# Two running sums in DRAM in place of three, for the routed rows of a mixture-of-experts layer

## The chip, the cores and the metric

The kernel runs on one core of one Trainium2 chip. The metric is device time in microseconds (us), the median of several executions. A core has five engines that run their own instruction streams and meet only at semaphores: TensorE (PE, with its weight loads as PEld), VectorE (DVE), ScalarE (ACT), GpSimd (POOL) and SyncE (SP), and 16 DMA engines that they all share.

## The reference

`x` has 32 batches of 100 rows of 256 numbers, 3200 tokens in all, float32. First a cross attention over a context of 361 rows of 192 is added to it. Then comes the part that matters here, a feed-forward layer with a router:

```
h = layernorm(x)
aff = softmax(h @ Wr + br)                  # 31 experts
vals, idx = top_k(aff, 3)
gates[token, expert] = vals where chosen, else 0
shared = gelu(h @ ws1 + bs1) @ ws2 + bs2
routed = sum over experts e of gates[:, e] * (gelu(h @ We1[e] + Be1[e]) @ We2[e] + Be2[e])
out = x + shared + routed + h
```

Each token has three experts. So 9600 rows have to be gathered by expert, multiplied, and added back to their tokens.

## The kernel before

**Attention stage.** Steps `i` from -2 to 36 run a pipeline over the 32 batches. For each finished tile of 128 tokens (25 tiles) it writes two rows per token into DRAM arrays of 3328 rows (3200 tokens and 128 rows for padding) of 256 floats: the residual into `sums[0]` (L370) and the normed row `h` into `sums[1]` (L371), both on SyncE's queue. GpSimd scatters `h` three times (L530) into `xs`, a DRAM array ordered by expert. At step 24 SyncE writes zeros from `pad_rows` into the whole of a third array, `sums[2]` (L349, one DMA of 3328 KB), and into the padding rows of the other two (L352, two DMAs of 128 KB). `spare_ready` counts these three.

**Routed stage.** 105 tiles of 128 rows, each of one expert, partly or wholly padding towards the end of the list. For each tile `t`:

- SyncE loads 128 rows with what belongs to them from `xs` into one of `XS = 6` buffers `xt` (L430), when `y_sb` of tile t-6 has been made.
- TensorE transposes them (L1176), forms the up product (L1187) and the down product (L1198), in the order transposes of t+2, up of t+1, down of t. ScalarE copies the transposed rows (L677) and applies gelu (L651).
- VectorE copies the token numbers of the rows to `token` (L934), fetches the weights of tile t+2 (L917), and evacuates the down product, scaled by the gate, to one of 6 `y_sb` buffers (L925). Before L934 it waits until the add of tile t-6 has landed (L933).
- GpSimd adds the 128 rows of `y_sb` to a sum in DRAM at the rows named in `token` (L552, an indirect DMA with `compute_op=ADD`). Sums are taken in turn. Two tiles of different experts can hold the same token, so the kernel never has two adds to one sum in flight: an add waits until the last add to the same sum has landed:

```python
s, sx = t.slot(3), t.slot(XS)
pool.wait_ge(token_ready, t.count(1))
pool.wait_ge(y_made, t.count(S_E + 1))
if t.has(3):
    pool.wait_ge(added[s], adds(t, 3))
alone(pool)
```

`alone` (L84) is a no-op that keeps these waits apart from the DMA instruction. After adds t = 1, 4, 7, ... up to 31, GpSimd also issues a plain DMA that pads the list of an expert (L559). SyncE issues 20 such pads (L416) between its loads.

**Tail.** When all adds have landed (L442), SyncE loads the sums in 11 groups of tiles (L448 to L450, one DMA of each sum for each group, into `part0`, `part1`, `part2`, which lie over the spent weights). VectorE adds the second and the third to the first (L959, L962). To tiles 0 to 7 it adds the shared expert's result, made early and kept in `tok` (L966). For the 17 others (`late_tiles`) TensorE forms the shared product after the routed tiles (L1106, L1115, L1116) into six PSUM banks, and VectorE adds it from there (L972). The product of late tile k from k = 6 on waits for the final sum of late tile k-6, whose bank it takes (L1223). After all loads are issued, SyncE writes the groups out (L453) as they are final.

Of the kernel before, what the change touches and what calls it, by code (L numbers as in the profile page):

```python
# [13 lines left out]
F32 = mybir.dt.float32  # L14
# [3 lines left out]
ALU = mybir.AluOpType  # L18
# [3 lines left out]
P = 128  # L22
B, LQ, LK = 32, 100, 361
D1, D2, E = 256, 192, 256
# [8 lines left out]
TOKENS = B * LQ  # L33
TILES = TOKENS // P
# [46 lines left out]
def alone(eng):  # L81


    eng.nop(nofuse=True)  # L84
# [18 lines left out]
GROUPS = [(8, 11), (0, 1), (11, 14), (1, 3), (14, 17), (3, 5), (17, 20), (5, 7), (20, 23), (7, 8), (23, 25)]  # L103


def starts(i):
    return FIRST.index(i) if i in FIRST else None


def ends(i):  # L110
    return LAST.index(i) if i in LAST else None


def batch(i):
    return i if 0 <= i < B else None
# [7 lines left out]
def program(nc, x, ctx_t, cols, rows, wqt, wkt, wvt, wo, bo, w1, be1, w2, b2, wr, br, out):  # L123
    xs = nc.dram_tensor("expert_rows_in", [LIST_END + P, ROW], F32, kind="Internal").ap()


    sums = [nc.dram_tensor(f"sum{k}", [TOKENS + P, D1], F32, kind="Internal").ap() for k in range(3)]
    flat_x = x.rearrange("b t d -> (b t) d")
    flat_out = out.rearrange("b t d -> (b t) d")

# [1 line left out]
    with stack:  # L132
        def sb(name, shape, dt=F32):
            return stack.enter_context(nc.sbuf_tensor(name, shape, dt))
# [7 lines left out]
        def sems(*names):  # L142
            return [stack.enter_context(nc.semaphore(n)) for n in names]

        XS = 6
        NT = ROUTED_TILES
        W = XS
        w1_all = sb("w1_all", [P, NE + 1, 2 * INTER])
        w2_all = sb("w2_all", [P, NE + 1, 2 * D1])
# [11 lines left out]
        pad_rows = sb("pad_rows", [P, ROW])  # L161
# [57 lines left out]
        token = ring(XS, "token", [P, 1], I32)  # L219
        own_exp, gate, inverse = two("own_exp", [P, TOP]), two("gate", [P, 1]), two("inverse", [P, 1])  # L220
        part0, part1 = w1_all[:, 0:TILES, 0:D1], w1_all[:, 0:TILES, D1:2 * D1]
        part2 = w2_all[:, 0:TILES, 0:D1]


        zt_ps0, zt_ps1 = bank[2], bank[3]
# [35 lines left out]
            "counts_made", "late_steps", "pads_ready", "pads_out", "pool_pads_out", "diag_made", "table_spread", "table_made",  # L261
            "gates_transposed", "gates_t_copied", "spare_ready")
        tile_in = sems(*[f"tile_in{s}" for s in range(XS)])
        added = sems("added0", "added1", "added2")
        (tile_transposed, tile_t_copied, w1_ready, up_made, act_made, down_made, y_made, token_ready, picked,
         inverse_made, gate_made) = sems(
            "tile_transposed", "tile_t_copied", "w1_ready", "up_made", "act_made", "down_made", "y_made", "token_ready",
            "picked", "inverse_made", "gate_made")
        rows_in = sems(*[f"rows_in{g}" for g in range(len(GROUPS))])
        third_in = sems(*[f"third_in{g}" for g in range(len(GROUPS))])  # L270
        sum_made, final_made, final_out = sems("sum_made", "final_made", "final_out")

        MADE = 23
# [21 lines left out]
        def cut(t):  # L295
            return slice(t * P, t * P + P)
# [12 lines left out]

        def adds(t, back=0):  # L310

            return t.turn(3, 1 - back // 3) * 16

        block = stack.enter_context(nc.Block())

# [1 line left out]
        def _(sp):  # L317
# [23 lines left out]
            def step(i):  # L341
                if batch(i + 4) is not None:
                    load_ctx(i + 4)
                if starts(i + 4) is not None:
                    load_x(starts(i + 4))
                if i == FILL_STEP:
                    sp.wait_ge(made, MADE)
                    alone(sp)
                    sp.dma_start(sums[2].rearrange("(k p) n -> p k n", p=P),  # L349
                                 pad_rows[:, 0:D1].unsqueeze(1).to_broadcast([P, TILES + 1, D1])).then_inc(spare_ready, 16)  # L350
                    for k in range(2):
                        sp.dma_start(sums[k][TOKENS:TOKENS + P, :], pad_rows[:, 0:D1]).then_inc(spare_ready, 16)  # L352
                    sp.dma_start(xs[LIST_END:LIST_END + P, :], pad_rows[:, :]).then_inc(pads_out, 16)
                if i == FILL_STEP + 2:
                    sp.dma_start(w1_all[:, NE, :], w1[NE]).then_inc(shared_in, 16)
                    sp.dma_start(w2_all[:, NE, :], w2[NE]).then_inc(shared_in, 16)
                if 1 <= i <= len(w1_order):
                    e = w1_order[i - 1]
                    sp.dma_start(w1_all[:, e, :], w1[e]).then_inc(expert_in, 16)
                if 1 <= i <= len(w2_order):  # L360
                    e = w2_order[i - 1]
                    if i == 1:
                        sp.wait_ge(folds_ready, 1)
                        alone(sp)
                    sp.dma_start(w2_all[:, e, :], w2[e]).then_inc(expert_in, 16)
                t = ends(i - 4)
                if t is not None:
                    sp.wait_ge(h_made, t + 1)
                    alone(sp)
                    sp.dma_start(sums[0][cut(t), :], resid[t % SLOTS][:, :]).then_inc(base_out[t % SLOTS], 16)  # L370
                    sp.dma_start(sums[1][cut(t), :], h_sb[t % SLOTS][:, 0:D1]).then_inc(h_out[t % SLOTS], 16)  # L371
# [66 lines left out]
            for t in range(FULL_FIRST, NT):  # L438
                load(At(0, t, W))

            for s in range(3):
                sp.wait_ge(added[s], len(range(s, NT, 3)) * 16)  # L442

            def rows_of(dram, lo, hi):
                return dram[lo * P:hi * P, :].rearrange("(k p) n -> p k n", p=P)

            for g, (lo, hi) in enumerate(GROUPS):
                sp.dma_start(part0[:, lo:hi, :], rows_of(sums[0], lo, hi)).then_inc(rows_in[g], 16)  # L448
                sp.dma_start(part1[:, lo:hi, :], rows_of(sums[1], lo, hi)).then_inc(rows_in[g], 16)
                sp.dma_start(part2[:, lo:hi, :], rows_of(sums[2], lo, hi)).then_inc(third_in[g], 16)  # L450
            for g, (lo, hi) in enumerate(GROUPS):
                sp.wait_ge(final_made, final_at[hi - 1])
                sp.dma_start(rows_of(flat_out, lo, hi), part0[:, lo:hi, :]).then_inc(final_out, 16)  # L453
# [3 lines left out]
        def _(pool):  # L457
            n = [0]

            def const(ins):  # L460
# [6 lines left out]
            k = const(pool.memset(tri[:, :], 1.0))  # L467
            pool.wait_ge(made, k)
            k = const(pool.affine_select(out=ident[:, :], in_=ident[:, :], compare_op=ALU.not_equal, fill=1.0,
                                         base=0, pattern=[[-1, P]], channel_multiplier=1))  # L470
# [24 lines left out]
            k = const(pool.memset(gates_all[:, TILES:28, :], 0.0))  # L495
# [42 lines left out]
            for s in range(SLOTS):  # L538
                pool.wait_ge(base_out[s], len(range(s, TILES, SLOTS)) * 16)
                pool.wait_ge(h_out[s], len(range(s, TILES, SLOTS)) * 16)  # L540
            pool.wait_ge(spare_ready, 48)

            def add(t):


                s, sx = t.slot(3), t.slot(XS)
                pool.wait_ge(token_ready, t.count(1))
                pool.wait_ge(y_made, t.count(S_E + 1))
                if t.has(3):
                    pool.wait_ge(added[s], adds(t, 3))  # L550
                alone(pool)
                pool.indirect_dma_start(sums[s], bass.IndirectOffsetOnAxis(ap=token[sx][:, 0:1], axis=0),  # L552
                                        y_sb[sx][:, :], None, compute_op=ALU.add).then_inc(added[s], 16)
# [140 lines left out]
        def _(dve):  # L694
# [233 lines left out]
            def tile(t, more=True):  # L928

                s, sx = t.slot(2), t.slot(XS)  # L930
                dve.wait_ge(tile_in[sx], t.turn(XS, 1) * 16)
                if t.has(XS):
                    dve.wait_ge(added[t.slot(3)], adds(t, XS))  # L933
                dve.tensor_copy(token[sx][:, :], xt[sx][:, TOKEN:TOKEN + 1]).then_inc(token_ready, 1)  # L934
                dve.scalar_tensor_tensor(own_exp[s][:, :], xt[sx][:, WHO:WHO + TOP], tile_e[:, t.r:t.r + 1],
                                         xt[sx][:, EXPS:EXPS + TOP], ALU.is_equal, ALU.mult).then_inc(picked, 1)
                dve.reciprocal(inverse[s][:, :], xt[sx][:, SUM:SUM + 1]).then_inc(inverse_made, 1)
                if more:
                    fetch_w1(t.back(-2))
                dve.wait_ge(picked, t.count(1))  # L940
                dve.tensor_reduce(gate[s][:, :], own_exp[s][:, :], AX.X, ALU.add).then_inc(gate_made, 1)
                evac(t)
# [14 lines left out]
            for g, (lo, hi) in enumerate(GROUPS):  # L957
                dve.wait_ge(rows_in[g], 32)
                dve.tensor_tensor(part0[:, lo:hi, :], part0[:, lo:hi, :], part1[:, lo:hi, :], ALU.add).then_inc(sum_made, 1)  # L959
                dve.wait_ge(sum_made, 2 * g + 1)  # L960
                dve.wait_ge(third_in[g], 16)
                dve.tensor_tensor(part0[:, lo:hi, :], part0[:, lo:hi, :], part2[:, lo:hi, :], ALU.add).then_inc(sum_made, 1)  # L962
                dve.wait_ge(sum_made, 2 * g + 2)
                if lo < S_E:
                    rows = part0[:, lo:hi, :].rearrange("p k (c q) -> p k c q", c=2)
                    dve.tensor_tensor(rows, rows, tok[:, :, lo * P:hi * P].rearrange("p c (k q) -> p k c q", q=P),  # L966
                                      ALU.add).then_inc(final_made, 1)
                else:
                    for t in range(lo, hi):
                        k = late_tiles.index(t)  # L970
                        dve.wait_ge(down_made, S_E + NT + k + 1)
                        dve.tensor_tensor(part0[:, t, :], part0[:, t, :], last_ps[k % 6], ALU.add).then_inc(final_made, 1)  # L972
# [299 lines left out]
```

## Time and profile before

| what | value |
|---|---|
| device time, median of 3 runs | 512.31 us (511.34 to 512.83) |
| span of the profiled execution | 515.6 us |
| PE busy | 473.5 us, 92% |
| POOL busy | 321.6 us, 62% |
| DVE busy | 349.8 us, 68% |
| adds L552 | 105, first at 262.3, last at 471.4 us |
| SyncE's wait at L442 for the last adds | 16.5 us |

The profiled execution is one execution, 3.3 us longer than the median of the unprofiled runs. Times in the views are counted from its first instruction. A share of busy time says little by itself: the three stages (attention up to some 242 us, routed tiles to 475 us, tail to 515.6 us) have different limits, and each is to be read for itself.

### The profile page before, as it was taken

What the parts mean: (1) busy time and instruction counts of PE and PEld (TensorE: products, weight loads), DVE (VectorE), ACT (ScalarE), POOL (GpSimd) and SP (SyncE); (2) the same over time, 40 slices, a digit from 0 to 9 for tenths busy, and PEclk for the clock granted to TensorE, in tenths of its full rate; (3) what the DMA queues carried; (4) which work ended last, traced back from release to release, by engine and by line L of the source; (5) the groups of instructions that cost most, each with busy time, mean ns of one, the idle gap of its engine ahead of it and who ended that gap; (6) DMA issues with size and microseconds to landing.
All of it is one profiled execution on the core that took longest, in us unless ns stands there. A gap on an engine that the chain in (4) does not pass through costs nothing.

```text
span 515.6 us, 13640 instructions
## 1 busy us (share of the span) xinstructions
PE 473.5 (92%) x3248; PEld 414.0 (80%) x3248; DVE 349.8 (68%) x1555; ACT 247.2 (48%) x823; POOL 321.6 (62%) x356
## 2 busy tenths in 40 slices
PE   8699888889888998888899999999999999999991
PEld 7577767778677787777799899989999999999891
DVE  4858787785878858657557666666666666661784
ACT  1455646465455555546255454454555555553220
POOL 3224856757565755657158888878888888885000
PEclk9899989999899889999999999999999999999996
DMA  7645767675555972569359999998998888875999
GB/s 238 178 145 180 244 211 231 219 231 181 190 181 166 348 246 93 165 203 329 90 121 186 190 183 179 191 151 135 138 137 143 138 135 137 137 117 65 350 350 316
DMA packets 81150, 97.53 MB, mean 189 GB/s; under 512 B 9201, under 2 KB 65906, under 8 KB 81074
## 3 DMA queue, kind: packets, MB, share of 16 engines
q1 hardware_dynamic: 60786, 70.79, 46.0%
q0 software_dynamic: 19248, 25.40, 29.6%
q10 hardware_dynamic: 1040, 0.48, 0.5%
q8 instruction: 29, 0.48, 0.4%
q14 instruction: 47, 0.39, 0.3%
HBM read 54.91 MB, written 41.73 MB: 187 GB/s over the span
## 4 chain that ended last, share of the span: by engine, by line
PE 49%; issue 15%; DVE 10%; DMA 8%; SPq 4%; POOL 3%; ACT 1%; POOLq 0%; DVEq 0%; another core or an unknown queue 0%
PE bank L1187 9%; PE bank L1198 9%; DMA sum<-y_sb,token 5%; POOL sum L552 3%; PE bank L1056 3%; PE bank L1045 3%; PE bank L1044 3%; PE bank L1176 2%; PE bank L1059 2%; PE bank L1083 2%; PE bank L1082 2%; DMA w_all<-sum 2%; DVE w_all L740 2%; PE bank L1031 2%; PE bank L1074 1%
## 5 line engine op out<-in xcount | busy, mean ns | idle before, releaser
L552 POOL DMA_INDIRECT sum<-y_sb,token x105 | 170.3, 1622 | 48.5 <-issue 26.7
L651 ACT ACTIVATE up<-bank,b_all 128x128 f32<-128x128 f32 x260 | 81.2, 363 | 103.0 <-PE bank L1187 44.8
L1187 PE MATMUL bank<-xtt,w1b 128*128 128x128 f32 x840 | 111.1, 275 | 0.3 <-ACT xtt L677 0.3
L1198 PE MATMUL bank<-w_all,up 128*128 x420 | 108.6, 381 | 0.0
L1187 PEld LDWEIGHTS bank<-xtt,w1b 128*128 128x128 f32 x840 | 102.1, 192 | 0.8 <-ACT xtt L677 0.5
L925 DVE TENSOR_SCALAR y_sb<-bank,gate,inverse 128x256 f32<-128x256 f32 x105 | 57.1, 544 | 53.5 <-PE bank L1198 27.5
L530 POOL DMA_INDIRECT expert_rows_in<-xt,slot x75 | 77.0, 1027 | 26.1 <-issue 20.7
L1198 PEld LDWEIGHTS bank<-w_all,up 128*128 128x128 f32 x420 | 71.7, 191 | 5.7
L917 DVE COPY w1b<-w_all 128x512 f32 x105 | 47.5, 452 | 19.1 <-issue 9.2
L677 ACT ACTIVATE xtt<-bank 128x256 f32<-128x256 f32 x105 | 40.1, 383 | 38.5 <-issue 21.4
L1176 PE MATMUL bank<-ident,xt 128*128 128x128 f32 x210 | 40.1, 274 | 0.4 <-DMA xt<-expert_rows_in 0.3
L1176 PEld LDWEIGHTS bank<-ident,xt 128*128 128x128 f32 x210 | 29.2, 141 | 12.0 <-DMA xt<-expert_rows_in 1.4
L608 ACT ACTIVATE tok<-bank 128x100 f32<-128x100 f32 x32 | 8.1, 253 | 58.2 <-PE bank L1059 52.1
L1056 PEld LDWEIGHTS bank<-w_all 128*128 128x128 f32 (+1 forms) x192 | 27.9, 200 | 10.1 <-issue 2.3
L505 POOL TENSOR_TENSOR rs<-mv,eps_cols 128x4 f32<-128x4 f32 x32 | 6.6, 207 | 45.1 <-DVE mv L777 44.7
L507 POOL TENSOR_TENSOR rs<-rs,mhalf 128x4 f32<-128x4 f32 x32 | 33.0, 1032 | 2.5
L740 DVE TENSOR_SCALAR w_all<-w_all,mv,rs 128x192 f32<-128x192 f32 x96 | 31.4, 384 | 1.6 <-POOL rs L507 1.3
L1044 PE MATMUL bank<-w_all,tok 128*100 128x361 f32 x64 | 27.7, 517 | 0.4 <-issue 0.4
L1056 PE MATMUL bank<-w_all 128*128 128x100 f32 (+1 forms) x192 | 27.0, 278 | 0.8 <-ACT w_all L589 0.8
L703 DVE BATCH_NORM_STATS2 c<-w_all 128x6 f32<-128x192 f32 x96 | 27.3, 341 | 0.0
L790 DVE RECIPROCAL rinv<-bank 128x1 f32<-128x1 f32 x25 | 4.2, 167 | 34.2 <-PE bank L1083 30.5
L1045 PE MATMUL bank<-w_all,tok 65*100 65x361 f32 x64 | 27.3, 510 | 0.0
(179 smaller groups left out, 939.1 us busy)
## 6 DMA issues: line engine op xcount, KB each, us to landing
xt<-expert_rows_in SPq DMA_DIRECT2D x105, 132.0 KB
w_all<-in_w SPq DMA_DIRECT2D x47, 256.0 KB
w_all<-in_ctx SPq DMA_DIRECT2D x32, 288.0 KB
w_all<-sum SPq DMA_DIRECT2D x15, 384.0 KB, 7.6
sum<-pad_rows SPq DMA_DIRECT2D x1, 3328.0 KB
w_all<-in_x SPq DMA_DIRECT2D x25, 128.0 KB, 2.9
sum<-y_sb SPq DMA_DIRECT2D x25, 128.0 KB
sum<-xt SPq DMA_DIRECT2D x25, 128.0 KB
```

Source lines behind the costliest of these rows:

```text
L530: pool.indirect_dma_start(xs, bass.IndirectOffsetOnAxis(ap=slot[s4][:, k:k + 1], axis=0), h_sb[s4][:, :], None).then_inc(scattered[s4], 16)
L552: pool.indirect_dma_start(sums[s], bass.IndirectOffsetOnAxis(ap=token[sx][:, 0:1], axis=0), y_sb[sx][:, :], None, compute_op=ALU.add).then ...
L651: ins = act.activation(up[s][:, m * P:m * P + P], up_ps[s][:, m * P:m * P + P], ACT.Gelu, bias=b1_all[:, e, m:m + 1].rearrange("p o n -> p ...
L740: ins = dve.tensor_scalar(z[s4][:, k, 0:D2], c_sb[s4][:, k, :], mv[s][:, k, 0:1], rs[s][:, 1, k:k + 1], ALU.subtract, ALU.mult)
L917: dve.tensor_copy(w1b[n.slot(2)][:, :], w1_all[:, bass.ds(e, 1), :].rearrange("p o n -> p (o n)"))\
L925: dve.tensor_scalar(y_sb[sx][:, :], down_ps[s], gate[s][:, 0:1], inverse[s][:, 0:1], ALU.mult, ALU.mult).then_inc(y_made, 1)
L1044: pe.matmul(bank[s][0:LQ, 0:LK], tok[:, 0, of_batch(b)], zt0[s], start=True, stop=False)
L1045: pe.matmul(bank[s][0:LQ, 0:LK], tok[0:D2C, 1, of_batch(b)], zt1[s], start=False, stop=True)\
L1056: pe.matmul(mix_ps[:, 0:LQ], z[s4][0:KT[k], k, 0:P], probs_t[s][0:KT[k], k, :], start=(k == 0), stop=(k == 2))
L1176: mm = pe.transpose(tile_ps[s][:, c * P:c * P + P], xt[sx][:, c * P:c * P + P], ident[:, :])
L1187: mm = pe.matmul(up_ps[s][:, m * P:m * P + P], w[:, c * INTER + m * P:c * INTER + m * P + P], xtt[s][:, c * P:c * P + P], start=(c == 0), ...
L1198: mm = pe.matmul(down_ps[s], up[s][:, m * P:m * P + P], w, start=(m == 0), stop=(m == 1))
```

## The change

The routed rows are added in turn to two sums, the one that begins as the residual and the one that begins as `h`. The third sum is neither allocated, filled with zeros, loaded nor added. The wait ahead of an add is now for the add two tiles back in place of three.

```diff
-    sums = [nc.dram_tensor(f"sum{k}", [TOKENS + P, D1], F32, kind="Internal").ap() for k in range(3)]
+    sums = [nc.dram_tensor(f"sum{k}", [TOKENS + P, D1], F32, kind="Internal").ap() for k in range(2)]
...
         def adds(t, back=0):
 
-            return t.turn(3, 1 - back // 3) * 16
+            return t.turn(2, 1 - back // 2) * 16
...
-                    sp.dma_start(sums[2].rearrange("(k p) n -> p k n", p=P),
-                                 pad_rows[:, 0:D1].unsqueeze(1).to_broadcast([P, TILES + 1, D1])).then_inc(spare_ready, 16)
                     for k in range(2):
                         sp.dma_start(sums[k][TOKENS:TOKENS + P, :], pad_rows[:, 0:D1]).then_inc(spare_ready, 16)
...
-            for s in range(3):
-                sp.wait_ge(added[s], len(range(s, NT, 3)) * 16)
+            for s in range(2):
+                sp.wait_ge(added[s], len(range(s, NT, 2)) * 16)
...
                 sp.dma_start(part1[:, lo:hi, :], rows_of(sums[1], lo, hi)).then_inc(rows_in[g], 16)
-                sp.dma_start(part2[:, lo:hi, :], rows_of(sums[2], lo, hi)).then_inc(third_in[g], 16)
...
-                s, sx = t.slot(3), t.slot(XS)
+                s, sx = t.slot(2), t.slot(XS)
                 pool.wait_ge(token_ready, t.count(1))
                 pool.wait_ge(y_made, t.count(S_E + 1))
-                if t.has(3):
-                    pool.wait_ge(added[s], adds(t, 3))
+                if t.has(2):
+                    pool.wait_ge(added[s], adds(t, 2))
...
                 if t.has(XS):
-                    dve.wait_ge(added[t.slot(3)], adds(t, XS))
+                    dve.wait_ge(added[t.slot(2)], adds(t, XS))
...
                 dve.tensor_tensor(part0[:, lo:hi, :], part0[:, lo:hi, :], part1[:, lo:hi, :], ALU.add).then_inc(sum_made, 1)
-                dve.wait_ge(sum_made, 2 * g + 1)
-                dve.wait_ge(third_in[g], 16)
-                dve.tensor_tensor(part0[:, lo:hi, :], part0[:, lo:hi, :], part2[:, lo:hi, :], ALU.add).then_inc(sum_made, 1)
-                dve.wait_ge(sum_made, 2 * g + 2)
+                dve.wait_ge(sum_made, g + 1)
```

## Rows read from the trace of the kernel before

**Rows 1.** The page: span, and busy time of TensorE and the rest.

```profile
span 515.6 us, 13640 instructions
PE 473.5 (92%) x3248; PEld 414.0 (80%) x3248; DVE 349.8 (68%) x1555; ACT 247.2 (48%) x823; POOL 321.6 (62%) x356
```

**Rows 2.** Windows: length, then busy us per engine (PE first), clock, DMA share, GB/s.

```profile
262.00:332.00 70.00, 69.57 (x485) 63.06 (x484) 45.97 (x207) 34.99 (x105) 59.60 (x44) 1.00 0.93 182
332.00:384.00 52.00, 51.97 (x368) 47.68 (x368) 34.91 (x159) 26.41 (x79) 42.82 (x27) 1.00 0.92 142
384.00:475.00 91.00, 91.00 (x639) 84.07 (x639) 55.28 (x257) 44.23 (x133) 74.72 (x46) 1.00 0.82 128
475.00:515.60 40.60, 29.80 (x187) 27.09 (x185) 25.45 (x44) 8.12 (x26) 0.00 (x0) 0.90 0.99 324
```

**Rows 3.** The chain that ended last (start, us, what): up products of two routed tiles.

```profile
361.89 0.89 PE bank L1187 x8
...
363.87 0.89 PE bank L1187 x8
```

**Rows 4.** All adds of L552: ns min/median/max, first and last start.

```profile
L552 POOL DMA_INDIRECT sum<-y_sb,token x105: 1543/1606/1797, 262.3 to 471.4; - x105
```

**Rows 5.** Timeline of DVE and POOL at the second add.

```profile
262.85 0.54 DVE L925 TENSOR_SCALAR y_sb<-bank,gate,inverse 128x256 f32<-128x256 f32 x1 [0.73 <-PE bank L1198]
...
264.21 1.57 POOL L552 DMA_INDIRECT sum<-y_sb,token  x1 [0.30 <-issue]
```

**Rows 6.** Timeline of POOL: adds after a gap, adds two before, and the last two.

```profile
345.42 1.71 POOL L552 DMA_INDIRECT sum<-y_sb,token  x1 [0.30 <-issue]
348.09 1.56 POOL L552 DMA_INDIRECT sum<-y_sb,token  x1 [0.96 <-DVE y_sb L925]
...
451.86 1.68 POOL L552 DMA_INDIRECT sum<-y_sb,token  x1 [0.30 <-DMA sum<-y_sb,token]
...
458.19 1.55 POOL L552 DMA_INDIRECT sum<-y_sb,token  x1 [0.69 <-issue]
...
469.53 1.55 POOL L552 DMA_INDIRECT sum<-y_sb,token  x1 [0.30 <-issue]
471.39 1.55 POOL L552 DMA_INDIRECT sum<-y_sb,token  x1 [0.30 <-issue]
```

**Rows 7.** The chain: adds from their start to the landing.

```profile
396.49 3.94 DMA sum<-y_sb,token
...
418.25 3.79 DMA sum<-y_sb,token
...
455.82 4.18 DMA sum<-y_sb,token
...
471.39 3.81 DMA sum<-y_sb,token
```

**Rows 8.** Timeline of SyncE's queue behind the fill of the third sum.

```profile
166.69 8.30 SPq L352 DMA_DIRECT2D sum<-pad_rows  x2
```

**Rows 9.** Windows around that fill, columns as in rows 2.

```profile
170.00:175.00 5.00, 3.81 (x31) 3.10 (x29) 3.94 (x23) 2.62 (x11) 4.10 (x6) 1.00 1.06 352
175.00:180.00 5.00, 4.96 (x24) 3.85 (x25) 4.27 (x22) 1.92 (x8) 3.75 (x5) 0.64 1.03 338
```

**Rows 10.** The chain near it: the same product at either clock.

```profile
176.34 1.06 PE bank L1044 x2
...
185.55 0.61 PE bank L1044 x2
```

**Rows 11.** The tail: timeline of SyncE's queue and DVE.

```profile
475.28 0.38 SPq L448 DMA_DIRECT2D w_all<-sum  x1
...
479.86 0.96 DVE L959 TENSOR_TENSOR w_all<-w_all 128x768 f32<-128x768 f32 x1 [11.05 <-DMA w_all<-sum]
...
482.25 1.08 DVE L972 TENSOR_TENSOR w_all<-w_all,bank 128x256 f32<-128x256 f32 x3
...
508.38 0.75 DVE L972 TENSOR_TENSOR w_all<-w_all,bank 128x256 f32<-128x256 f32 x2
```

More of the change, by code:

```diff
@@ L221, in program @@
         part0, part1 = w1_all[:, 0:TILES, 0:D1], w1_all[:, 0:TILES, D1:2 * D1]
-        part2 = w2_all[:, 0:TILES, 0:D1]
         zt_ps0, zt_ps1 = bank[2], bank[3]
@@ L263, in program @@
         tile_in = sems(*[f"tile_in{s}" for s in range(XS)])
-        added = sems("added0", "added1", "added2")
+        added = sems("added0", "added1")
         (tile_transposed, tile_t_copied, w1_ready, up_made, act_made, down_made, y_made, token_ready, picked,
@@ L269, in program @@
         rows_in = sems(*[f"rows_in{g}" for g in range(len(GROUPS))])
-        third_in = sems(*[f"third_in{g}" for g in range(len(GROUPS))])
         sum_made, final_made, final_out = sems("sum_made", "final_made", "final_out")
@@ L540, in _ @@
                 pool.wait_ge(h_out[s], len(range(s, TILES, SLOTS)) * 16)
-            pool.wait_ge(spare_ready, 48)
+            pool.wait_ge(spare_ready, 32)
             def add(t):
-                s, sx = t.slot(3), t.slot(XS)
+                s, sx = t.slot(2), t.slot(XS)
                 pool.wait_ge(token_ready, t.count(1))
                 pool.wait_ge(y_made, t.count(S_E + 1))
-                if t.has(3):
-                    pool.wait_ge(added[s], adds(t, 3))
+                if t.has(2):
+                    pool.wait_ge(added[s], adds(t, 2))
                 alone(pool)
```

## The prediction

> **What bounds the kernel now.** I read the windows by stage first, since an average over three stages says nothing about one. TensorE is busy for 92% of the span [rows 1] and for all but 0.5 us of the 213 us of the routed stage, at full clock [rows 2]. The chain of waits confirms it: one routed tile is one turn of TensorE, 363.87 - 361.89 = 1.98 us [rows 3]. The adds keep the same pace: (471.39 - 262.3) / 104 = 2.01 us apart [rows 4, 6]. From 375 us on the chain runs over GpSimd instead, because the last add's landing is what the tail waits for. The tail is bound by transfers, DMA share 0.99 at 324 GB/s, with TensorE busy 29.8 of 40.6 us [rows 2].
>
> So the question is what the adds' queue can do when an add has to wait for the add two back. Two numbers decide it, the time from an add's start to its landing and the time from a release to the next start.
>
> **The loop of one sum.** Landing: the chain shows seven adds from start to landing, 3.79 to 4.18 us, mean 3.9 [rows 7]. This contains the 1.55 us that the instruction occupies GpSimd [rows 6]. Restart: the second add found GpSimd idle and waited only for `y_sb`, made at 262.85 + 0.54 = 263.39; it began at 264.21, 0.82 us later [rows 5]. A wait for a landing sits at the same place, ahead of the no-op, so I take 0.82 us for it too. Before the change this is hidden: one sum comes up every 3 x 1.98 = 5.94 us, and the loop needs 3.9 + 0.82 = 4.72. It shows only when a landing is late. The add at 458.19 comes late after even spacing, and three turns earlier the add began at 451.86 [rows 6]; if the landing released it, that landing took 458.19 - 0.82 - 451.86 = 5.51 us. The gap before 348.09 is of the same kind. Such gaps are rare, so most landings stay below 5.94 - 0.82 = 5.1 us, which is the upper bound where the chain shows none.
>
> After the change one sum comes up every 2 tiles, 3.96 us at TensorE's pace, and the loop needs 4.72. The loop becomes the bound: 4.72 / 2 = 2.36 us per tile. GpSimd's own limit, 471.39 - 469.53 = 1.86 us [rows 6], stays below, and the eleven plain pads among the early adds fit into the new idle time of about 0.5 us (partly).
>
> The seven landings lie in a window with DMA share 0.82; from 262 to 384 us it is 0.93 and 0.92 [rows 2], and no landing there is in the chain. Bounds: 3.8 us, the shortest seen, and 5.1. I take 4.2: busier engines lengthen it, yet two adds in flight in place of up to three, and a fifth fewer loads per us, shorten it. About 60 adds start there, so their pace is (4.2 + 0.82) / 2 = 2.51 us; the other 44 intervals take 2.36.
>
> Last add: 262.3 + 60 x 2.51 + 44 x 2.36 = 516.7. It lands 3.81 later [rows 7], at 520.5, against 471.39 + 3.81 = 475.2. **Routed stage: +45.3 us.**
>
> What is late next: VectorE's copy of `token` for tile t waits for the landing of add t-6, and everything behind it on that engine with it (weights of t+2, evacuation). TensorE runs out of `y_sb` buffers some six tiles in and then idles 2.4 - 1.98, about 0.5 us per tile. SyncE's load of tile t+6 waits for the same evacuation. None of these adds time: evacuation follows the landing by some 2 us, and four adds are still queued then, 4 x 2.4 us of work.
>
> At this place the Trainium skill (DMA: Bandwidth & Descriptors, section Anatomy of one DMA) gives 2.0 us plus bytes / 436 GB/s for a DMA of GpSimd, 2.3 us for these 128 KB, as an estimate. Taken as the whole loop it would hide the wait. The trace's 3.8 to 4.2 us from the start of the instruction speak against that reading: the 1.55 us on GpSimd come first.
>
> **The fill removed.** One DMA of 3328 KB disappears at 166 us, and the 8.3 us for which SyncE is held up behind it [rows 8]. I cost it at nothing. The DMA engines are full at 170 to 180 us [rows 9], but the chain there runs over TensorE and VectorE without a DMA in it. What could be gained: TensorE's clock is 0.64 on average in the window after it was busy for 3.81 of 5 us [rows 9], and the same product takes 1.06 in place of 0.61 us [rows 10]. If the fill had a part in that idling, its absence gives back up to 0.36 x 5 + 0.3 x 5, some 3 us. I keep 0 to -3, and take 0 because the chain names none of its transfers.
>
> **The tail.** 11 of 33 loads go, 3.28 of 9.83 MB. At the 350 GB/s of these transfers (352 at full share, [rows 9]) that is 9.4 us, the upper bound, as transfers fill the tail. VectorE's 11 third additions, under 1 us each (the first group's is seen between 479.86 and 482.25), go too. But then TensorE's late tiles hold the end. First loads are issued at 475.28, the first addition starts at 479.86, and the first final tile at 482.25 [rows 11], of which 0.96 + some 0.4 us belong to the third sum: after the change it comes at landing + 5.7. From there TensorE has eleven down products of 1.3 us and nine up products of 0.9 left, 22.3 us (eight matmuls of 128 columns take 0.89 us [rows 3], which is the up product; the down product with its bias has six of 256 columns, at twice the time each, 1.3). Then the last addition, about 0.8, and the last write: now 515.6 - 509.1 = 6.5 us after the last addition's end at 508.38 + 0.75 [rows 11], when the writes queue. Sum: 5.7 + 0.4 + 22.3 + 0.8 + 6.5 = 35.7 us against 515.6 - 475.2 = 40.4. With an emptier queue the last write may be 2 to 3 us shorter; but TensorE will have stood still for some 10 us before (six late tiles, 13 us, fit ahead of the landing and are done early) and may start at the low clock, costing about as much. **Tail: -5 us**, bounds -3 and -9.4.
>
> **Sum.** +45.3 - 5 + 0 = +40.3. Against its own execution: 515.6 + 40.3 = 555.9. The median of the runs is 3.3 us below the profiled execution, so 512.3 + 40.3 = 552.6 us.
>
> **The rivals.**
>
> *The clock falls in the routed stage.* TensorE will be busy for 1.98 of 2.44 us, 81%. The window with 76% ended in the low level, 1.2 GHz for part of the next stretch [rows 9]. At 1.2 GHz a tile costs 3.96 us. Short stretches of it are hidden by the four queued adds; if the mean clock came to 0.75, a tile would cost 1.98 / 0.75 = 2.64 us, and the stage 104 x (2.64 - 2.45) = 20 us more: 573 us. Against it: after the drop TensorE has no idle time, so the clock should recover. The Trainium skill (TensorE: Matmul & The Clock Gate, section The HAM clock gate) says that idleness lowers the clock and activity releases it, which could make it swing. Chance 0.10.
>
> *Landings get much shorter.* With fewer adds in flight all could land in 3.8 us or just below: 104 x 2.31 = 240.2, last add at 502.5, +31.1; with a tail of -9.4 it gives +21.7, 534 us. For it speaks that the last add, with no loads beside it, took 3.81; against it that this was no shorter than others. Chance 0.12.
>
> *Faster: the wait stays covered.* The routed stage keeps its 1.98 us, only the tail shows: 512.3 - 5 = 507 us (503 at best). This needs a loop under 3.96 us, so a landing of 3.14 after 0.82; with 5 us from the tail the balance is at 1.98 + 5/104 = 2.03 us per tile, a landing of 3.24. The shortest in the trace is 3.79 [rows 7]. Or the restart costs nothing, because the queue of GpSimd runs ahead: then (3.9 + 0) / 2 = 1.95, covered. Against this speaks the 0.82 us at 264.21 and the late add at 458.19, which fits a landing within the range only with some restart. Chance 0.04.
>
> *Landings as long as the middle of the bounds*, 4.5 early and 4.1 later: 60 x 2.66 + 44 x 2.46 = 267.8, +58.7, tail -3: 568 us. Chance 0.12.
>
> **How the numbers follow.** My forecast has 0.62, its rivals 0.10, 0.12, 0.04 and 0.12. The range takes in short and middle landings, 535 to 570 us, and leaves the clock and the covered wait outside. A measurement tells 0.3%, 1.5 us, from no change; slower by more 0.96, within 0.01, faster 0.03 (the covered wait's 0.04, in two parts).
>
> **What would show it.** The adds L552 spaced 2.3 to 2.6 us, GpSimd idle over 0.7 us before each, released by the add two back; TensorE some 80% busy from 280 us on; VectorE's L934 waiting for a landing; last add near 517 us; a tail of 34 to 37 us with TensorE in it, idle just before the landing. The prediction is wrong if adds stay 2 us apart (restart or landing hidden), if the clock column shows 0.8 or less in the routed stage, or if the stage before 250 us moves by more than 3 us.

## The result, and the profile after

The changed kernel takes 555.69 us (median of 4 runs, 553.15 to 559.36) against 511.82 us of the kernel before on the same chip: ratio 1.0823, 95% interval 1.0741 to 1.0906. It is slower by 43.9 us. The forecast was 552.6 us, 40.3 us more, with a range of 535 to 570. A second chip repeats the ratio (1.0854, 1.0785 to 1.0923), at absolute times that differ by chip.

The page of the changed kernel, beside [rows 1]. The last two lines are the head of its chain of waits, by engine and by line.

```profile
span 557.7 us, 13607 instructions
PE 492.5 (88%) x3248; PEld 421.1 (76%) x3248; DVE 346.0 (62%) x1544; ACT 248.3 (45%) x823; POOL 316.0 (57%) x356
...
PEclk9789989989899989999999999999999999999989
...
PE 34%; DMA 31%; issue 11%; DVE 10%; SPq 2%; ACT 1%; POOL 1%; DVEq 1%; POOLq 1%; another core or an unknown queue 0%
DMA sum<-y_sb,token 30%; PE bank L1036 3%; PE bank L1048 3%; PE bank L1037 3%; PE bank L1107 3%; PE bank L1051 2%; PE bank L1098 2%; PE bank L1074 2%; PE bank L1023 2%; DVE w_all L735 1%; PE bank L1088 1%; PE bank L1075 1%; PE bank L984 1%;
```

DMA transfers now hold 31% of the chain, and 30% of the span is one thing, the way of an add from its start to its landing. The windows by stage answer to [rows 2]; the columns are the same.

```profile
262.00:332.00 70.00, 64.24 (x428) 56.25 (x426) 40.50 (x180) 31.13 (x93) 46.90 (x36) 1.00 0.76 150
332.00:384.00 52.00, 45.89 (x302) 40.11 (x303) 30.06 (x129) 21.55 (x64) 35.68 (x24) 1.00 0.73 131
384.00:516.00 132.00, 116.83 (x766) 102.02 (x765) 71.66 (x316) 53.79 (x160) 84.39 (x54) 1.00 0.66 105
516.00:524.00 8.00, 8.00 (x52) 7.38 (x51) 0.00 (x0) 2.51 (x8) 4.66 (x3) 1.00 0.57 66
524.00:557.70 33.70, 25.19 (x147) 22.56 (x145) 17.34 (x33) 6.26 (x20) 0.00 (x0) 0.90 0.89 292
```

TensorE is busy for 64.24, 45.89 and 116.83 us of 70, 52 and 132, 89% in place of 100%. Its granted clock stays at 1.00 in all of the routed stage, the higher of the two levels. The DMA share fell from 0.93, 0.92 and 0.82 to 0.76, 0.73 and 0.66. So neither an engine nor the transfers are full: the stage is bound by a latency.

All adds of the changed kernel, beside [rows 4], and then its timeline of GpSimd, beside [rows 6]:

```profile
L547 POOL DMA_INDIRECT sum<-y_sb,token x105: 1544/1552/1839, 264.5 to 520.7; - x105
```

```profile
356.62 1.55 POOL L547 DMA_INDIRECT sum<-y_sb,token  x1 [0.90 <-DVE token L929]
358.83 1.55 POOL L547 DMA_INDIRECT sum<-y_sb,token  x1 [0.66 <-DVE token L929]
361.28 1.55 POOL L547 DMA_INDIRECT sum<-y_sb,token  x1 [0.90 <-DVE token L929]
363.42 1.55 POOL L547 DMA_INDIRECT sum<-y_sb,token  x1 [0.59 <-DVE token L929]
365.99 1.55 POOL L547 DMA_INDIRECT sum<-y_sb,token  x1 [1.02 <-DVE token L929]
367.97 1.55 POOL L547 DMA_INDIRECT sum<-y_sb,token  x1 [0.43 <-issue]
370.49 1.55 POOL L547 DMA_INDIRECT sum<-y_sb,token  x1 [0.97 <-DVE token L929]
```

(520.7 - 264.5) / 104 = 2.46 us from add to add, against 2.01. Every second add belongs to the same sum, 356.62, 361.28, 365.99, 370.49, so a turn takes 4.5 to 4.7 us. The view names VectorE's copy of `token` as the releaser. That is a trap: the token of tile t+4 waits for the same landing as add t, so its copy runs at the very moment at which the add is released. The add's own inputs were ready long before: by the trace's records, from the seventh add on its rows had been made over 4.1 us earlier and its own token copied over 6.0 us earlier. The chain of the changed kernel takes it apart, in order of time (start, us, what):

```profile
508.12 5.28 DMA sum<-y_sb,token
513.40 0.02 issue
513.42 0.02 POOLq L545
513.44 0.04 issue
513.48 0.04 POOLq L84
513.52 0.69 issue
514.21 3.79 DMA sum<-y_sb,token
518.00 0.02 issue
518.03 0.02 POOLq L545
518.04 0.04 issue
518.09 0.04 POOLq L84
518.13 0.69 issue
518.82 1.04 POOL sum L547
```

The landing at 513.40 lets the wait at L545 pass at once. The no-op follows, then 0.69 us until the add starts at 514.21: 0.81 us from landing to start. Then 3.79 us to the next landing, and 0.82 us again. These two terms and nothing else make up one turn.

**Where the 42.1 us of the profiled executions went** (557.7 - 515.6). The first add starts 2.2 us later (264.52 against 262.30). The 104 intervals take 256.2 in place of 209.1 us, 47.1 more. The tail, from the last landing to the end, takes 557.7 - 524.4 = 33.3 in place of 40.4 us, 7.1 less. 2.2 + 47.1 - 7.1 = 42.2.

The tail in the timeline of the changed kernel, beside [rows 11]:

```profile
524.42 0.38 SPq L444 DMA_DIRECT2D w_all<-sum  x1
...
528.98 0.96 DVE L954 TENSOR_TENSOR w_all<-w_all 128x768 f32<-128x768 f32 x1 [17.49 <-DMA w_all<-sum]
...
529.97 1.08 DVE L964 TENSOR_TENSOR w_all<-w_all,bank 128x256 f32<-128x256 f32 x3
530.45 2.07 PE L1107 MATMUL bank<-w_all,up 128*128 128x256 f32 x4 [5.52 <-DVE w_all L964]
...
534.44 1.03 PE L1107 MATMUL bank<-w_all,up 128*128 128x256 f32 x4
...
544.69 0.42 DVE L964 TENSOR_TENSOR w_all<-w_all,bank 128x256 f32<-128x256 f32 x1 [1.77 <-PE bank L1108]
...
554.74 0.42 DVE L964 TENSOR_TENSOR w_all<-w_all,bank 128x256 f32<-128x256 f32 x1 [0.80 <-PE bank L1108]
```

The first final tile begins at 529.97, 5.6 us after the landing. TensorE had run out of free banks and stood still for 5.52 us; its four matmuls at 530.45 then take 2.07 us, and 1.03 at 534.44. The windows show the clock of that stretch, and of the rest (columns as in [rows 2]):

```profile
524.93:530.45 5.52, 0.00 (x1) 0.00 (x1) 1.44 (x3) 0.63 (x2) 0.00 (x0) 0.70 0.88 292
530.45:534.00 3.55, 3.55 (x11) 3.01 (x12) 3.13 (x8) 0.00 (x0) 0.00 (x0) 0.51 1.09 353
534.00:557.70 23.70, 20.70 (x130) 18.80 (x128) 12.78 (x24) 5.64 (x18) 0.00 (x0) 1.00 0.89 295
```

The granted clock fell to the lower level, 1.2 GHz, while TensorE stood still, and was back at the higher one from 534 us on. From 544 us on VectorE waits for TensorE before its final additions, 1.77 us at 544.69, so this end of the tail is held by TensorE, no longer by transfers. The last addition ends at 555.16, and the last write is done 2.6 us later.

### The profile page after: what moved, and what is told of

The parts are those of the page before. It is cut to its first block, busy times and chain, and to the rows that moved or that the text cites. A ratio compares the mean times of both kernels' runs of the same rounds, so it can differ in the third digit from the quotient of the medians.

```text
span 557.7 us, 13607 instructions
## 1 busy us (share of the span) xinstructions
PE 492.5 (88%) x3248; PEld 421.1 (76%) x3248; DVE 346.0 (62%) x1544; ACT 248.3 (45%) x823; POOL 316.0 (57%) x356
## 4 chain that ended last, share of the span: by engine, by line
PE 34%; DMA 31%; issue 11%; DVE 10%; SPq 2%; ACT 1%; POOL 1%; DVEq 1%; POOLq 1%; another core or an unknown queue 0%
DMA sum<-y_sb,token 30%; PE bank L1036 3%; PE bank L1048 3%; PE bank L1037 3%; PE bank L1107 3%; PE bank L1051 2%; PE bank L1098 2%; PE bank L1074 2%; PE bank L1023 2%; DVE w_all L735 1%; PE bank L1088 1%; PE bank L1075 1%; PE bank L984 1%; PE bank L983 1%; PE bank L1108 1%
## 5 line engine op out<-in xcount | busy, mean ns | idle before, releaser
L547 POOL DMA_INDIRECT sum<-y_sb,token x105 | 164.8, 1570 | 100.7 <-DVE token L929 81.6
L1179 PE MATMUL bank<-xtt,w1b 128*128 128x128 f32 x840 | 115.2, 280 | 26.9 <-DVE w1b L912 20.5
L1190 PE MATMUL bank<-w_all,up 128*128 x420 | 110.1, 385 | 0.2
L929 DVE CAST token<-xt 128x1 int32<-128x1 f32 x105 | 15.7, 149 | 32.6 <-DMA sum<-y_sb,token 31.7
L1107 PE MATMUL bank<-w_all,up 128*128 128x256 f32 x100 | 27.0, 394 | 5.9 <-DVE w_all L964 5.5
L1036 PE MATMUL bank<-w_all,tok 128*100 128x361 f32 x64 | 29.0, 539 | 0.0
```

What stands on the lines that cost most here:

```text
L1036: pe.matmul(bank[s][0:LQ, 0:LK], tok[:, 0, of_batch(b)], zt0[s], start=True, stop=False)
L1107: pe.matmul(to, up[s][:, m * P:m * P + P], w2_all[:, NE, m * D1:(m + 1) * D1], start=(m == 0), stop=False)
L1179: mm = pe.matmul(up_ps[s][:, m * P:m * P + P], w[:, c * INTER + m * P:c * INTER + m * P + P], xtt[s][:, c * P:c * P + P], start=(c == 0), ...
L1190: mm = pe.matmul(down_ps[s], up[s][:, m * P:m * P + P], w, start=(m == 0), stop=(m == 1))
```

## The experiments

All were compared with the kernel before on their own chip; its median was 499.3 us on the chip of e1, e2 and e4, 500.7 on that of the repeated changed kernel, e5 and e6, 498.6 on that of e7 to e9 and 516.9 on that of e10 and e11. Where a mean landing is given, it comes from the trace's records of landings. An add is counted as landed when the last of its 16 parts is.

**e1, the wait alone.** Three sums, with fill and loads, but an add waits for the add two back:

```diff
-                if t.has(3):
-                    pool.wait_ge(added[s], adds(t, 3))
+                if t.has(2):
+                    pool.wait_ge(added[(t.r - 2) % 3], ((t.r - 2) // 3 + 1) * 16)
```

> The kernel before with all three sums, their fill and their loads, but an add waits for the landing of the add two tiles back. Theory (the wait is the cost, 2.0 to 2.45 us per tile, and the third sum's work in the tail is worth 5 to 7 us): slower than the changed kernel by those 5 to 7 us, 559 to 565 us, ratio to before 1.09 to 1.10; adds L552 2.4 to 2.5 us apart; tail from the last landing some 40 us as before. Rival (two arrays in place of three make the adds themselves slower, by sharing rows or memory): 510 to 515 us, adds 2.0 us apart.

Measured: 549.71 us, ratio 1.0984 (1.0921 to 1.1048), 50.4 us slower. All adds of this kernel:

```profile
L552 POOL DMA_INDIRECT sum<-y_sb,token x105: 1543/1552/1758, 246.5 to 508.6; - x105
```

(508.6 - 246.5) / 104 = 2.52 us. One line of code that moves no byte costs more than the whole change. That two arrays make adds slower in themselves is refuted: with three arrays and the same wait they come as far apart. Against the changed kernel's 1.0854 on another chip (below) this one is 0.013 slower, 6.5 us, the third sum's work in the tail.

**e2 and e4, the savings alone.** e2 leaves out the third loads and additions in the tail, and e4 leaves out the fill as well; adds stay three deep. In both the third's part of the routed rows is missing in the output.

```diff
-                sp.dma_start(part2[:, lo:hi, :], rows_of(sums[2], lo, hi)).then_inc(third_in[g], 16)
...
-                dve.wait_ge(third_in[g], 16)
-                dve.tensor_tensor(part0[:, lo:hi, :], part0[:, lo:hi, :], part2[:, lo:hi, :], ALU.add).then_inc(sum_made, 1)
```

> The kernel before with three sums, three adds deep, but the third is neither loaded nor added in the tail, so the third's part of the routed rows is missing in the output. Theory (TensorE's late tiles and the transfers of the two others hold the tail at 33 to 36 us): 505 to 508 us, ratio 0.986 to 0.991. Rival A (the tail is bound by TensorE alone, the transfers were hidden): 510.5 us, gain under 2 us. Rival B (bound by transfers alone): 502.9 us, gain 9.4 us.

> As the kernel without the third load, and the fill of the third sum is left out too: all that the change saves, without the wait that it adds. The third's part of the routed rows is missing in the output. Theory (the fill is hidden): within 1.5 us of the kernel without the third load. Rival (the fill slows the attention stage, by its queue or by the clock that fell behind it): 2 to 4 us faster than that kernel. The difference between the changed kernel and this one is the price of the wait: 46 to 49 us.

Measured: e2 492.43 us, ratio 0.9858 (0.9814 to 0.9902); e4 493.06 us, ratio 0.9868 (0.9827 to 0.9908). The third sum's work in the tail is worth 6.9 us, at the upper end of the theory's range and between the two rivals. The fill is worth nothing: without it the kernel was 0.6 us slower, which the intervals do not tell from zero. e4 is the changed kernel without its wait, and the repeated changed kernel, below, has 1.0854. The wait costs 1.0854 - 0.9868 = 0.0986 of some 500 us, 49 us; e1 gave 50.

**The changed kernel again, e5 and e6: what the landing consists of.**

> The changed kernel again, as a base for the next two on the same chip. Ratio to before 1.075 to 1.09.

Measured: 542.54 us, ratio 1.0854 (1.0785 to 1.0923).

e5 makes the add a plain write of the same rows, so most of the routed part is missing in the output:

```diff
-                                        y_sb[sx][:, :], None, compute_op=ALU.add).then_inc(added[s], 16)
+                                        y_sb[sx][:, :], None).then_inc(added[s], 16)
```

> The changed kernel with the 105 adds made plain row writes (the last writer of a row keeps it, so most of the routed part is missing in the output), same bytes, same waits. Theory A (the landing is mostly a fixed price of a DMA that GpSimd issues, whatever it does at the row): landing 3.5 to 3.9 us, period 2.3 to 2.45 us, time within 8 us of the changed kernel. Rival B (reading each row before writing it is what takes the time): landing 3.0 us or less, period at TensorE's 1.98 us, and the time near that of the kernel without the wait, 45 us under the changed kernel.

Measured: 491.03 us, ratio 0.9815 (0.9748 to 0.9882), 51.5 us below the repeated changed kernel. Its adds:

```profile
L547 POOL DMA_INDIRECT sum<-y_sb,token x105: 954/960/1215, 243.9 to 455.2; - x105
```

They occupy GpSimd for 0.96 us in place of 1.55 and come (455.2 - 243.9) / 104 = 2.03 us apart, TensorE's pace, with the same wait in the code. The mean from start to landing is 3.00 us, against 4.04 in the repeated changed kernel. Theory A is wrong: adding in place of writing costs 1.04 us of the landing, 0.59 of it already on GpSimd and some 0.45 after it. Rival B had the size right, but its reason, that each row has to be read first, is not shown: more than half of the price lies in GpSimd's instruction, and the rest was not taken apart. A window of e5, beside the one from 332 to 384 us in [rows 2]; the columns are the same:

```profile
314.00:366.00 52.00, 52.00 (x369) 47.91 (x368) 34.27 (x159) 26.28 (x78) 26.78 (x27) 1.00 0.49 144
```

TensorE is full again, so 1.04 us of landing is the whole difference between a wait that is hidden (3.00 + 0.82 = 3.82, under 3.96) and one that costs 50 us. It is only just hidden: 70 of 103 adds still start within 0.9 us of the landing that they wait for. The rows show one thing more: at the same rate of bytes, 142 and 144 GB/s, the DMA engines are busy for 0.92 of the time with adds and 0.49 with plain writes. So 0.43 of the 0.92 go with the adding.

e6 adds only 128 of the 256 columns, to arrays of their own, which the tail does not read (the routed part is missing in the output):

```diff
-                                        y_sb[sx][:, :], None, compute_op=ALU.add).then_inc(added[s], 16)
+                                        y_sb[sx][:, 0:P], None, compute_op=ALU.add).then_inc(added[s], 16)
```

> The changed kernel with adds of 128 of the 256 columns, to arrays of their own (the routed part is missing in the output). Half the bytes, the same 128 rows and waits. If the bytes set the landing, it falls from 3.9 to some 3.2 us and the period to 2.1 us, 30 us less. If it is fixed by rows and by the DMA's start and end, landing 3.6 to 3.8 us and 5 to 10 us less.

Measured: 521.74 us, ratio 1.0425 (1.034 to 1.051), 20.8 us below the repeated changed kernel. Its adds:

```profile
L549 POOL DMA_INDIRECT half<-y_sb,token x105: 1543/1552/1778, 243.3 to 482.7; - x105
```

(482.7 - 243.3) / 104 = 2.30 us apart, in the same 1.55 us of GpSimd each, since the number of rows is the same. Mean landing 3.57 us, 0.47 less than with whole rows. It fell between the two expectations: half of the bytes is worth 0.47 of 4.04 us, and the 3.57 that are left, with 0.82 for the restart, are still too long for a loop of 3.96 us.

**e7, e10, e11: a start for the tail before the last landing.** The kernel before with all three sums. SyncE waits for each sum by itself and loads its first groups (`AHEAD` = 4, 2 or 1) while the other sums still take their last adds:

```diff
+            for s in order:
+                sp.wait_ge(added[s], len(range(s, NT, 3)) * 16)
...
+                for g in range(AHEAD):
+                    part_in(s, g)
+            for g in range(AHEAD, len(GROUPS)):
+                for k in range(3):
+                    part_in(k, g)
```

> The kernel before, all three sums, but in the tail SyncE waits for each sum by itself: the first four groups of a sum are loaded as soon as its last add has landed, 3.7 and 1.9 us before the last add of all. If the transfers bind the tail, it ends 1.5 to 3 us earlier, ratio 0.994 to 0.997. If TensorE's late tiles hold the end through the first final tile, the first group of the third sum still comes last and later than now, behind eight other loads: no gain or 1 to 2 us slower.

Measured with four groups: 497.89 us, ratio 0.9973 (0.9943 to 1.0003), an interval that takes in no change. In its timeline of VectorE the second and the third sum of the first group come 3.46 us apart:

```profile
461.59 0.96 DVE L970 TENSOR_TENSOR w_all<-w_all 128x768 f32<-128x768 f32 x1 [11.31 <-DMA w_all<-sum]
465.05 0.96 DVE L973 TENSOR_TENSOR w_all<-w_all 128x768 f32<-128x768 f32 x1 [2.50 <-DMA w_all<-sum]
```

The third sum's first group is loaded behind eight others and comes late, as the second expectation said. Fewer groups early should cure that:

> As the kernel with four groups loaded early, with two groups (4 tiles, 512 KB of each sum, 1.5 us of transfer, which fits between two landings 1.86 us apart). The first group of the third sum comes with its landing and the first final tile no later than before. If the order was what cost the version with four groups its gain: 2 to 3 us faster than before, ratio 0.994 to 0.996. If the tail isn't bound by transfers at its start, no gain.

> The same with one group (3 tiles, 384 KB of each sum) early: 1 to 2.5 us faster than before, ratio 0.995 to 0.998, and the first final tile 1 to 2 us earlier after the last landing than before.

Measured: two groups 513.63 us, ratio 0.9949 (0.9908 to 0.9989), 2.6 us faster than the kernel before on that chip; one group 516.10 us, ratio 1.0003 (0.9957 to 1.0048), nothing. With two groups the same pair comes 2.84 us apart, and the first final tile begins at 478.26:

```profile
474.43 0.96 DVE L970 TENSOR_TENSOR w_all<-w_all 128x768 f32<-128x768 f32 x1 [9.48 <-DMA w_all<-sum]
477.27 0.96 DVE L973 TENSOR_TENSOR w_all<-w_all 128x768 f32<-128x768 f32 x1 [1.88 <-DMA w_all<-sum]
478.26 1.08 DVE L983 TENSOR_TENSOR w_all<-w_all,bank 128x256 f32<-128x256 f32 x3
```

The landing records show what none of the expectations had: the early loads slow the very add that they are to overtake. The last add takes 3.81 us to land before, 5.05 with one group early, 5.89 with two and 6.72 with four (5.57 in e9, which has four as well). Counted from the start of the last add, the first final tile comes after 10.86 us before, and after 9.64, 10.52 and 13.15; the end comes after 44.2 us before, and after 43.4, 43.8 and 41.8. So in these profiled executions, one of each kernel, four groups early have the latest first tile and yet the shortest tail. The first final tile doesn't settle the end, and the cause of the different gains stays open.

Of the versions that leave no work out, the one with two groups alone beat the kernel before by more than its interval, and by little (0.9989 at its upper end). The three intervals overlap, so they do not say which number of groups is best.

**e8 and e9, the pads moved.** GpSimd issues 11 pads between its adds; e8 gives them to SyncE, one after each load from tile 4 on, and e9 has the early loads of four groups besides.

```diff
-        PADS_SP, PADS_POOL = range(0, 20), range(20, NE)
+        PADS_SP, PADS_POOL = range(0, NE), range(NE, NE)
...
-                if t >= 4 and t % 2 == 0 and (t - 4) // 2 < len(PADS_SP):
+                if t >= 4 and t - 4 < len(PADS_SP):
```

> The kernel before, with the 11 pads of GpSimd's queue moved to SyncE's. The last add began 2.6 us after its rows were made, and GpSimd's backlog was built by these pads, so the last landing comes up to 1.7 us earlier: ratio 0.996 to 0.998, and adds in the first 70 us of the stage 1.98 us apart in place of 2.08. Rival: the pads delay SyncE's loads of the next tiles, and TensorE waits for one more than once: no gain or slower.

> Both edits on the kernel before. If both gains hold, they add up to 3 to 5 us, ratio 0.990 to 0.994.

Measured: e8 507.34 us, ratio 1.0152 (1.0112 to 1.0193); e9 504.43 us, ratio 1.0102 (1.0062 to 1.0142). Both slower. The waits of e8 between 240 and 330 us (engine, line, waited for; us in total, times, longest):

```profile
PEld bank L1175 <- DMA xt<-expert_rows_in: 13.0, 17, 2.2
...
PE bank L1175 <- DMA xt<-expert_rows_in: 6.3, 11, 1.8
```

The rival was right: with a pad after each load TensorE's weight loads wait 17 times, 13.0 us, for rows. In e7, on the same chip and with the pads where they were, they wait 6 times in the same window, 2.3 us. The adds of the first 60 tiles come 2.17 us apart, not 1.98 as expected, against 2.05 before. An idle GpSimd was bought with a late SyncE. e9 takes back 2.9 us of it, but the 3 to 5 us of gain expected of it did not come, since the gain of the pads did not.

## Why the prediction was right, point by point

- **The loop of one sum becomes the bound.** Right, and shown: e1 has the wait alone and costs 50.4 us, e4 has all but the wait and gains 6.2. The loop's terms stand in the chain of the changed kernel, 3.79 and 0.82 us.
- **Restart 0.82 us.** Right as the shortest: 62 of 103 adds start within 0.9 us of the landing that they wait for. But the mean over all is 1.02 us. I had left out that two sums share GpSimd: a landing can find it at work on the other sum's add, and then it waits. The adds at 518.82 and 520.68 are such a pair, 1.86 us apart, which is GpSimd's own limit, in place of 2.46. The mean of 1.02 is somewhat too high, as this trace has all 16 records of a landing for 43 of the 105 adds alone. The repeated changed kernel has them for all: mean 0.93 us, 79 of 103 within 0.9. Of the 24 others, 8 follow the add before within 1.95 us and 6 follow a pad, which are 5.1 us late in sum: the pads did not quite fit into the idle time.
- **Landing 4.2 us early and 3.9 later.** By the records that this trace has, 3.99 and 3.82; by the complete ones of the repeated kernel, 4.10 and 3.95. So the early landing was 0.1 to 0.2 us too long. Before the change the records give a mean of 4.46 early and 4.05 later: the seven landings of the chain, mean 3.9, were not typical, and it was right to go above them. The error in the landing and that in the restart cancel: 4.2 + 0.82 and 3.99 + 1.04 (or 4.10 + 0.95) are all 5.0 to 5.1. The pace came out as 2.51 early, as forecast, and 2.39 later, forecast 2.36. That the sum is so exact is partly luck. The routed stage is +47.1 against +45.3.
- **The tail, -5 us.** The right sign and mechanism, the size too small: -7.1 in the profile, 6.9 by e2. The terms were sized as follows. First final tile 5.6 us after the landing (forecast 5.7). TensorE's idle time before it 5.5 us, not some 10, with the low clock after it, as said. TensorE's remaining work took 24.2 us (530.45 to 554.7) against 22.3, which is the low clock's 1.9. The mis-sized term is the last write: 2.6 us, where I kept the 6.5 of before. I had set this gain and the low clock against each other one for one; they are 3.9 and 1.9. The bound of 9.4 us took 350 GB/s from another stretch; at the 324 GB/s of the tail itself [rows 2] it would have been 10.1.
- **The fill at nothing.** Right within the noise: e4 against e2 is 0.6 us the other way, with intervals of some 2 us to either side.
- **The rivals.** The clock in the routed stage stayed at 1.00 with TensorE 89% busy, so that rival did not occur. I had put the busy share at 81%. By work it is 1.98 / 2.46 = 80%; the view counts more because the records of successive matmuls overlap and cover part of the gaps. In e1, with its adds at the same pace, the clock did fall once in the routed stage: its mean is 0.51 from 486.5 to 490.0 us and 1.00 after that. So such a drop can occur here, though far from the mean of 0.75 that the rival needs. The covered wait did not occur, but it was nearer than its chance of 0.04 says: e5 shows that an operation 1.04 us shorter is covered. The short landings did not come either, with 3.8 us only in the later part and restarts above 0.82.
- **The stage before the first add** is 2.2 us longer in this execution. e2 and e4 differ by 1.1 us in the same place without any reason in the code (first adds at 243.9 and 245.0). The granted clock goes with it: its mean up to 240 us is 0.94 in the changed kernel and 0.96 before, and 0.99 in e2 and e4. I take it for scatter between executions; it was not tested further.

## What to carry to other kernels

A ring of n accumulators (or buffers) hides a latency only up to n times the period: before taking one away, compare (landing + restart) with (n - 1) periods, for the mean and not only for the best case. Here 4.9 us, 2 x 2.46, stands against 4.0 after the change, and 5.1 stood against 6.0 before it. The 0.9 us per turn of two tiles became 47 us over 105 tiles, against 7 us saved once. The restart has to be in the sum, and so does the engine that issues for all members of the ring.

## What the runs showed of the hardware

- From the landing of a DMA to the start of the next DMA instruction on an idle GpSimd queue, which waits for it ahead of a no-op, 0.81 to 0.82 us pass (chain of the changed kernel). SyncE's first load starts 0.02 us after the landing that it waits for (524.40, 524.42).
- An adding scatter of 128 rows of 1 KB takes 1.55 us of GpSimd and 4.04 us to land; a plain scatter of the same rows 0.96 and 3.00 us; an adding one of half rows 1.55 and 3.57 us. Adding in place of writing, 1.04 us, weighs more than half of the bytes, 0.47. The Trainium skill (DMA: Bandwidth & Descriptors, Anatomy of one DMA) gives 2.0 us plus bytes / 436 GB/s, as an estimate from it 2.3 us for whole rows and 2.15 for half. Counted from the end of the instruction on GpSimd, the runs agree within 0.3 us: 2.49 for the add, 2.04 for the plain write, 2.02 for half rows.
- At the same rate of bytes (142 and 144 GB/s) adding scatters keep the DMA engines busy for 0.92 of the time and plain ones for 0.49 (the kernel before, e5).
- The mean landing is 4.49 us with adds three deep (e4, DMA share 0.96, 0.91 and 0.85 by window) and 4.08 us with adds two deep on the same chip (e1, DMA share 0.81, 0.74 and 0.66); the repeated changed kernel has 4.04. Some 0.4 us of a landing are contention. Whether with the other adds or with the other transfers, which are fewer per us too, was not separated.
- An add of 128 KB that lands in 3.81 us by itself takes 5.05 to 6.72 us with loads of 384 to 1152 KB of each finished sum beside it (the last add of the kernel before, and of e11, e10, e9 and e7).
- The attention stage differs between chips: the changed kernel's first add starts at 264.5 us with a mean granted clock of 0.94 up to 240 us, and in the repeated run on another chip at 241.9 us with 1.00. That is as much as half of the effect studied here, so only ratios on one chip were used.
